# An expert's PSUM bank freed one engine earlier, SELU's result laid out in order of time, and four mixing steps moved forward in a five-stage audio tower

## The reference, cut to what matters

```python
# token stage
w = softmax(logits)                                  # 31 taps, 4 heads
y = einsum("bthk,btkhd->bthd", w, xg) + bias         # the "mixing" by bands
z = selu(conv1d(y, Wc) + bc)                         # 128 -> 512 channels, 31 taps
h = z @ W2.T + b2
# first mixture: all 8 experts, weighted by comb
h1 = silu(einsum("td,ehd->teh", xf, w1))
eo = einsum("teh,edh->ted", h1, w2)
routed = einsum("te,ted->td", comb, eo)
```

## Time and profile before

| what | us |
|---|---|
| median of 3 runs (lowest to highest) | 2265.41 (2263.96 to 2266.24) |
| the profiled execution, its own time | 2269.88 |
| its span, first to last instruction | 2268.1 |
| TensorE busy | 1861.0 |
| VectorE busy | 1404.4 |
| ScalarE busy | 977.4 |
| GpSimd busy | 866.4 |

### The profile page before, as it was taken

How to read it: one execution, slowest core, us unless ns; L and a number is a source line. 1 busy time by engine, 2 the same in 40 slices (tenths; PEclk the granted TensorE clock), 3 DMA queues, 4 the chain that set the end, 5 groups by cost and what they waited for, 6 DMA issues and landing times.

```text
span 2268.1 us, 47779 instructions
## 1 busy us (share of the span) xinstructions
PE 1861.0 (82%) x17168; PEld 1501.3 (66%) x17168; DVE 1404.4 (62%) x4603; ACT 977.4 (43%) x2557; POOL 866.4 (38%) x750
## 2 busy tenths in 40 slices
PE   3688999999999999999998999999978777166660
PEld 2576777877777787878786878787755555144430
DVE  4784465767667766767676766666665757344440
ACT  2353454545454636454645454544535441021110
POOL 1000011113343425251524262434334356768885
PEclk9999999999999999999999999999989898577775
DMA  6773754534344333433342423233200001067765
GB/s 210 270 255 119 264 170 140 168 114 118 109 124 140 109 104 116 125 91 118 92 145 58 138 79 124 64 119 98 79 5 7 7 4 26 8 121 120 117 89 73
DMA packets 167562, 251.52 MB, mean 111 GB/s; under 512 B 67362, under 2 KB 122981, under 8 KB 166577
## 3 DMA queue, kind: packets, MB, share of 16 engines
q10 hardware_dynamic: 43656, 153.58, 21.1%
q0 software_dynamic: 56672, 51.14, 10.5%
q1 hardware_dynamic: 67016, 43.91, 7.4%
HBM read 203.03 MB, written 87.40 MB: 128 GB/s over the span
## 4 chain that ended last, share of the span: by engine, by line
PE 43%; issue 21%; POOL 12%; DMA 9%; DVE 7%; ACT 5%; ACTq 1%; POOLq 0%; SPq 0%; DVEq 0%
PE W L1038 17%; PE Cb L1038 17%; POOL slots_dram L952 8%; DMA odd_sum_dram<-qv 5%; PE L L1038 4%; PE W L1211 3%; DMA out<-qv 3%; POOL h L945 2%; PE L L1066 1%; ACT xh L1539 1%; POOL odd_sum_dram L1018 1%; DMA ring<-filters_dram 1%; DMA band<-band_dram 1%; ACT conv_s L1504 1%; ACT seq_hi L1466 1%
## 5 line engine op out<-in xcount | busy, mean ns | idle before, releaser
L1038 PE MATMUL Cb<-seq_hi,ring 128*128 128x174 f16 x4356 | 572.8, 240 | 20.6 <-DVE seq_lo L1769 10.4
L1038 PE MATMUL Cb<-seq_lo,ring 128*128 128x174 f16 x2178 | 506.5, 240 | 0.0
L952 POOL DMA_INDIRECT slots_dram<-rows,slot_i x384 | 457.4, 1191 | 111.0 <-issue 111.0
L1038 PEld LDWEIGHTS Cb<-seq_hi,ring 128*128 128x128 f16 x4356 | 386.6, 98 | 51.9 <-DVE seq_lo L1769 11.1
L945 POOL TENSOR_TENSOR h<-h,xh 115x384 f32<-115x384 f32 x120 | 120.1, 1001 | 707.1 <-ACT xh L1539 706.9
L1583 ACT ACTIVATE area_k<-W 115x345 f32<-115x345 f32 x384 | 176.5, 460 | 331.7 <-PE W L1211 316.9
L2007 DVE SCALAR_TENSOR_TENSOR area_h<-area_h,W 128x345 f32<-128x345 f32 x256 | 131.4, 514 | 236.6 <-ACT area_h L1529 207.4
L2100 DVE CUSTOM_DVE_ANT_0 area_h<-W,offsets 115x345 f32<-115x345 f32 x384 | 196.4, 513 | 113.3 <-PE W L1038 103.5
L1038 PE MATMUL W<-area_k,qv 64*115 64x345 f16 (+1 forms) x1920 | 253.4, 381 | 14.8 <-POOL h L945 8.8
L1211 PE MATMUL W<-ident,area_h 115*115 115x115 f32 x1152 | 197.3, 281 | 72.5 <-POOL h L945 51.2
L1577 ACT ACTIVATE area_h<-area_h,nmax 115x345 f32<-115x345 f32 x384 | 224.8, 585 | 31.0 <-DVE nmax L2100 30.5
(11 more groups left out here) (270 smaller groups left out, 3069.0 us busy)
## 6 DMA issues: line engine op xcount, KB each, us to landing
ring<-filters_dram ACTq DMA_DIRECT2D x252, 512.0 KB
slots_dram<-in_empty_slots POOLq DMA_DIRECT2D x8, 1544.0 KB, 14.6
area_k<-slots_dram SPq DMA_DIRECT2D x64, 193.0 KB
filters_dram<-ring ACTq DMA_DIRECT2D x24, 512.0 KB, 4.4
band<-band_dram SPq DMA_DIRECT2D x64, 189.0 KB
filters_dram<-offsets ACTq DMA_DIRECT2D x12, 512.0 KB, 4.3
slots_dram<-rows,slot_i POOLq DMA_INDIRECT x384
x_win<-in_xpad SPq DMA_DIRECT2D x16, 252.0 KB
```

Of the source, the lines that this page charges most:

```text
L952: pool.indirect_dma_start(out=slots_d, out_offset=bass.IndirectOffsetOnAxis(ap=slot_i[parity(b)][:, m:m + 1], axis=0), in_=rows[parity(b)] ...
L1038: return pe.matmul(o, l, r, start=start, stop=stop)
```

## The change

Three edits. First, a `Y` bank of expert e < 8 counts as freed when ScalarE has scaled it (`y_scaled`) and no longer when GpSimd has added the result; the last iteration, where VectorE reads the bank itself, keeps the old signal. Second, `selu` is laid out in order of time; VectorE writes it in that order, and TensorE takes its 115 weights with a step of three float32 elements (12 bytes). Third, `MIX_AT` puts parts 5, 6 and 7 of the mixing at projection points 8, 10 and 11 instead of 9, 11 and 13.

```diff
-MIX_AT = {r: n for n, r in enumerate([1, 2, 4, 5, 7, 9, 11, 13])}
+MIX_AT = {r: n for n, r in enumerate([1, 2, 4, 5, 7, 8, 10, 11])}
@@
+SCALED = [("Y", e) for e in range(E0)]
@@
-        A1 = PH * M // J
-        selu = sb("selu", [128, OC, J, 2 * A1])
+        selu = sb("selu", [128, OC, 2, PH * M])
@@ wait_freed
             name, k, behind = FREED[prev]
+            if prev in SCALED and (ago or ro.kind != "last"):
+                name = "y_scaled"
             sig = named[name]
             eng.wait_ge(sig.h, sig.at(back(ro.b, ago + behind), k))
@@ tok_out on TensorE
-   last = mm(bank[0:A, j * C:(j + 1) * C], selu[:, o, j, r * A1:r * A1 + A], w2T[:, o, :],
+   last = mm(bank[0:A, j * C:(j + 1) * C], selu[:, o, r, j:j + J * (A - 1) + 1:J], w2T[:, o, :],
@@ conv_event on VectorE
-   dve.scalar_tensor_tensor(selu[:, o, :, :].rearrange("p j n -> p n j"),
-                            zn.rearrange("p b (a j) -> p (b a) j", j=J), -1.0,
-                            z.rearrange("p b (a j) -> p (b a) j", j=J),
-                            ALU.add, ALU.add).then_inc(selu_ready.h, 1)
+   dve.scalar_tensor_tensor(selu[:, o, :, :], zn, -1.0, z, ALU.add, ALU.add).then_inc(selu_ready.h, 1)
```

## The result

The changed kernel takes 2242.44 us (median of 4 runs, 2240.95 to 2244.22), the kernel before, beside it, 2264.68 us (4 runs, 2263.17 to 2266.24). The ratio is 0.9902, 95% interval 0.9885 to 0.9919: faster by 22 us, 1.0%. The forecast was 2219 us, 46 us faster. The time lies inside the forecast's range of 2203 to 2243 us, but less than half of the forecast 46 us came.

A forecast was written before the change was run, and what follows sets the result against it. TensorE's own instructions were taken to set the time from 300 to 1660 us, a ring of handovers from 1660 to 1866. Terms -39 - 4.9 - 2.3 = -46.2 us from 2265.4 gave 2219 us, 8-in-10 range 2203 to 2243.

The forecast's parts named there:

- edit 2: SELU in order of time: 2.3 us gained, no cost for 384 `tok_out` weight loads with 12-byte step, far bound 8 us.
- rival D: Stepped weight load 1.5 times slower: +21 on the sum, 2240 us, chance 0.05; second form three times, 2303 us, chance 0.03.
- rival B: TensorE's waits change name to ScalarE or VectorE; edit 1 gives -19 us, edits 2 and 3 halved; 2243 us, chance 0.17.
- the forecast's row: Another instruction's loads: four of 126 columns at 16-byte step in 0.58 us, six of 128 neighbouring in 0.74; 0.12-0.13 against 0.11 each.
- near -25 us by that rule: By 16-byte SBUF lines, three of four accesses at 12 bytes open a new line; slower loads, sum near -25 us.
- Edit 1, the bank: TensorE's 60.0 us of waits for GpSimd's add shrink 47.5, less 3.7 and 4.7: -39 us, bounds -47.5 and -15.
- the end of each pair: Long wait where ScalarE goes into copies of the next pair's sequences; seven places, half of 1.07 us each struck, 3.7 us.
- The waits for VectorE's `nmax` at the turns: TensorE arriving sooner meets VectorE less ready; 12.8 us of waits before, taking back a tenth of 47.5, 4.7 us.
- Edit 3, the mixtures: Earlier mixing removes 7.3 us of waits for `y` before `tok_logits`, adds 2.4: -4.9 us, bounds -7.3 and 0.
- new waits for `area_b`: Two more products per sequence one point behind their turn: waits about double, 4.8 us from 300 to 1660 us.
- Edit 2, VectorE's side: SELU add 0.56 us shorter, 32 times; little on TensorE's path, 2.3 us gained, bounds 0 and 18.
- The marks set in the forecast: Profile signs: run at 1013.90 about 19 us sooner, under 9 means B; 48 loads over 6 us, D; maxima waits beyond 20.

The follow-up runs named there:

- set B: One chip, against before: changed kernel -28.3 us; it with neighbouring weights -49.8 or 8-byte step -51.8; old SELU layout, add in planes' order -47.0.
- set D: One chip, against before: kernel before unaltered +0.9 us; bank's release alone -40.2; changed kernel -28.9; old SELU layout with add in planes' order -48.2.
- set C: One chip, against before: changed kernel with old SELU -40.2 us, neighbouring weights -50.8, 16-byte step -13.1; planes'-order add with `zn` in planes' order too -32.8.
- set A: One chip, edits made in the kernel before, against before: bank alone -33.2 us, SELU alone +12.3, mixtures alone -3.4, bank and mixtures together -34.5.

## Why the prediction was wrong

**The step that failed.** It is in edit 2: "I take no cost, and 0.02 x 384 = 8 us as the far bound on that side by this row." The load with a step of 12 bytes costs 0.05 us more, 2.36 us for each pair of the full stretch, and 20.7 us in the kernel (set B). This is rival D in its first form, which had been priced right (21 us on the sum) and given a chance of 0.05. With it alone the sum would have been 46.2 - 20.7 = 25.5 us, against the 22 us of the first comparison and the 28 to 29 of sets B and D. The first comparison's 2242.4 us is also what rival B gave (2243), but by chance: B had the bank's edit at -19 us, and it is -33.2 and -40.2 by itself.

Why the row misled: the forecast compared the pace of two runs of loads, four with a step of 16 bytes in 0.58 us and six without in 0.74. That pace is real, but it is the pace of another instruction's loads. The last four loads of a run of `tok_out`, in the trace of before and in set C's kernel with the same step of 16 bytes (views from 800 us on), are

```profile
799.87 0.51 PEld L1038 LDWEIGHTS Cb<-w2T,selu 128*115 128x115 f32 x4
```

```profile
799.71 0.94 PEld L1042 LDWEIGHTS Cb<-w2T,selu 128*115 128x115 f32 x4
```

0.51 us with neighbouring columns and 0.94 with the step, against the 0.58 of the transposes. A load of the transposes has 96 partitions and 126 columns, one of `tok_out` has 128 and 115 and belongs to an ordinary float32 product; which of these differences makes the step cheap in the first no run tells. The duration of single loads would have warned, but it would not have given the price either. In the trace of before, the stepped loads of the forecast's row, its six neighbouring ones, other neighbouring ones of 128 columns, and neighbouring ones of 115 columns are

```profile
L1066 PEld LDWEIGHTS L<-ident,band x256: 193/218/230, 26.7 to 1382.8; 96*126 96x126 f32 x128
```

```profile
L1038 PEld LDWEIGHTS L<-xT,winT x96: 186/192/338, 413.6 to 1931.1; 128*128 128x128 f32 x96
```

```profile
L1198 PEld LDWEIGHTS W<-ident,xh x96: 138/140/251, 192.4 to 1879.2; 115*128 115x128 f32 x96
```

```profile
L1211 PEld LDWEIGHTS W<-ident,area_h x1152: 175/179/318, 217.1 to 1865.1; 115*115 115x115 f32 x192
```

218 ns against 192, 140 or 179: 1.14, 1.56 or 1.22 times, by which neighbour one takes, while the neighbours differ among themselves. Measured at the shape in question, 12 bytes cost 245/179 = 1.37 times and 16 bytes 1.72. So the row held some penalty but not its size, and 0.02 us a load was no bound for `tok_out`. VectorE's 1.5 times on a 16-byte step, which gave the forecast its 0.055 us for rival D, was nearer to the 0.05 measured.

The page of the Trainium skill that the forecast weighed ("Advanced Engine Details and Errata", section "Memory Cachelines": 16-byte lines in SBUF, full speed needs at least two hits on a line) holds for the loads of `tok_out`. Counted out by its rule, steps of 4 and 8 bytes are free, 12 bytes pays in part, and 16 pays at every element; the loads took 179, 185, 245 and 308 ns. The transposes' stepped loads, 218 ns and four in 0.58 us, agree with it only in part. The forecast's own sentence, near -25 us by that rule, is where the kernel landed.

**Edit 1, the bank.** The mechanism and the size were right: -39 forecast, -40.2 in set D, -33.2 in set A. Of the full stretch the forecast had 32.7 less 8.4 taken back, 24.3 us, and set D has 24.1 in its six pairs. What is taken back is spread otherwise than the text had it. The place that it named, the end of each pair, gives back nearly all of its gain and not half. There ScalarE makes the exp of the next turn behind its copies of the next pair's sequences, so the next turn waits longer by what the first one gained. In the trace of before (first two rows, to be read behind the earlier trace rows) and in the changed kernel the two turns are

```profile
1007.45 0.53 PE L1211 MATMUL W<-ident,area_h 115*115 115x115 f32 x3 [2.01 <-POOL h L945]
...
1008.80 0.93 PE L1211 MATMUL W<-ident,area_h 115*115 115x115 f32 x3 [0.38 <-ACT area_h L1577]
```

```profile
998.27 0.53 PE L1215 MATMUL W<-ident,area_h 115*115 115x115 f32 x3 [0.56 <-ACT xh L1543]
...
1000.70 0.56 PE L1215 MATMUL W<-ident,area_h 115*115 115x115 f32 x3 [1.46 <-ACT area_h L1581]
```

From 300 to 1660 us the waits for `area_h` at the turns are 2.2 us over 6 times in the kernel before and 8.4 over 6 in the changed one. That is 6.2 us where the forecast struck 3.7. The waits for VectorE's `nmax` at the turns, where it had 4.7, did not grow in the first trace (12.8 in both) and by 1.2 us in set D (12.8 and 14.0 with the bank alone). The sum of the two came out right because one was too small and the other too large.

**Edit 3, the mixtures.** The wait for `y` went, as forecast. The new waits for `area_b` did not come: 2.4 us over 10 times from 300 to 1660 us in both kernels, where 4.8 were expected. Yet the gain is 3.4 us alone and 2.3 on top of the bank, both too small to be told from nothing; -4.9 is inside the first interval. The term was small and its sign was not measured with certainty. Of the 7.3 us of waits that went, the six pairs of set A show 2.3 (1283.2 and 1280.9 us, on top of the bank); where the rest went is not shown.

**Edit 2, VectorE's side.** 2.3 us forecast, 10.4 measured (set C), inside its bounds of 0 and 18. The forecast counted only products that wait for `selu`, and of setup 1.4 us. It is a term mis-sized, most of it ahead of the full stretch (set C), and how much of that is the jump of some us between executions is open. It hid part of the error of the load: 20.7 - (10.4 - 2.3) = 12.6 us of net error in edit 2.

**The account.** Where the chip is that of sets B and D: -40.2 (bank) - 2.3 (mixtures) - 10.4 (add) + 20.7 (load) = -32.2 us from terms of four sets, and -28.3 and -28.9 measured. The six pairs, free of setup, add up more closely: -24.1 - 2.3 - 2.4 + 13.9 = -14.9 us, and 1278.3 - 1292.6 = -14.3 measured in set D. In set A: -33.2 - 2.3 and +12.3 for SELU give -23.2, and the first comparison had -22.

**The marks set in the forecast.** Waits for the add gone, `xh` at 12.5 us: 11.2. No wait over 0.95: 0.9. SELU add 0.87 us: 0.88. The 48 loads in 5.3 us: 7.66, which was the mark for D. The run of loads at 1013.90 about 19 us sooner: it starts at 1005.95, 8 us sooner. The forecast read less than 9 us as B; but four runs of loads lie before it, three of them 2.36 us and the one in setup 1.56 us longer, and without them it would be 16.6 us sooner. Waits for VectorE's maxima beyond 20 us: 16.5 + 3.0 = 19.5, and they were 16.5 + 4.4 = 20.9 before. Two marks that can be set off by one another's cause should have been made apart.

## What to carry to other kernels

Where a run of weight loads sets TensorE's pace, the bytes between its columns are part of its price: take it from loads of the same shape and the same kind of product, or measure it with one run on neighbouring weights; four loads of another instruction with a step of 16 bytes took 0.58 us here, four of this one 0.94. A stepped access is better kept on an engine that has slack, but a low share of busy time is not enough to show slack: ScalarE is busy 45% of the time, and 0.7 us more in each of 32 passes went with a loss of about 14 us. A loop order in which the output is written by neighbours and the inputs are read with a step was the cheaper half of a transposing copy here. When a bank's content has been taken, free it by the engine that took it and not by the one that uses the result.

## What the hardware showed that was not expected

The penalty of a step in a weight load of 115 float32 columns: 179, 185, 245 and 308 ns at 4, 8, 12 and 16 bytes. Up to 8 bytes the step is nearly free, and the two further elements of step add 60 and 63 ns. Neighbouring float32 loads are not all alike either: 179 ns for 115 columns, 140 and 192 ns for two groups of 128.

VectorE's add of 696 columns takes 882 ns with neighbours throughout, 1118 with both inputs at 12 bytes, 1121 with one of them, and 1436 with the output jumping from plane to plane; ScalarE's pass with such an output, and neighbouring input, goes from 875 to 1583 ns.

The same program differs between chips by more than a chip's own runs do: bank and mixtures took 2236.96 us in set A and 2220.18 in set C, the kernel before 2271.93 and 2259.34. One place can be seen. In the trace of the changed kernel from the first comparison, ScalarE's copy of the turned weights starts 0.74 us after the turn that it waits for has ended:

```profile
995.33 0.47 PE L1215 MATMUL W<-ident,area_h 115*115 115x115 f32 x3
...
996.54 0.46 ACT L1587 ACTIVATE area_k<-W 115x345 f32<-115x345 f32 x1 [1.71 <-PE W L1215]
```

The same two instructions in set D's trace of it, with a gap of 0.03 us:

```profile
987.95 0.47 PE L1215 MATMUL W<-ident,area_h 115*115 115x115 f32 x3
...
988.45 0.46 ACT L1587 ACTIVATE area_k<-W 115x345 f32<-115x345 f32 x1 [1.00 <-PE W L1215]
```

In the first trace TensorE idles 0.82 us before the product that follows. The view of waits from 300 to 1660 us of the first trace has

```profile
PE W L1042 <- issue: 4.2, 5, 0.9
```

five idle times for which the view names no releaser, the 0.82 us among them; set D's view has no such row. Why ScalarE comes late there stays open, and it is less than half of the 10 us by which the six pairs are longer in the first trace (1288.3 against 1278.3); the kernel before is longer there by 4.4 us as well (1297.0 against 1292.6).
